# First attention of a two-layer model: scores and maxima on column tiles of 32

## The chip, the cores and the metric

The kernel runs on one core of a Trainium2 chip. The metric is device time in microseconds (us) of one execution, the median of several. TensorE multiplies matrices, VectorE (DVE) reduces and combines, ScalarE (ACT) does exponentials and copies, GpSimd (POOL) small work, and SyncE (SP) issues most DMAs. TensorE's results go to PSUM, which has 8 banks of 128 partitions x 512 f32.

## The reference, cut to what matters

The model has two layers; the change lies in the first layer's attention, over 4 batches of 1024 tokens, 16 heads of 8 dimensions.

```python
zn = (z - mu) / jnp.sqrt(var + EPS) * ln_scale + ln_bias
qkv = zn @ w_qkv
...
scores = jnp.einsum('bhqd,bhkd->bhqk', q, k) / SCALING      # SCALING = 8 ** 0.5
att = jax.nn.softmax(scores, axis=-1)
out = jnp.einsum('bhal,bhlv->bhav', att, v)
out = jnp.transpose(out, (0, 2, 1, 3)).reshape(b, n, d)
out = out @ w_proj + b_proj
return z + out
```

So there are 64 score matrices (4 batches x 16 heads) of 1024 x 1024. Behind this stand a gate, a second layer with a landmark attention and an iterated inverse, and a mixture of eight experts.

## The kernel before

**Operands.** q and k are each split into three bf16 parts; a product of scores is a bf16 matmul whose contraction runs over all nine pairs of parts (ROWS = 72 rows, 9 x 8). A tile of q or k, `q0[c]` or `k0[c]` (b_q, b_k), holds four heads (a "quad") with 96 rows; three slots c take turns. Rows 72 to 74 of q hold the negated row maxima, as three bf16 parts, against rows of ones in k, so that the matmul of scores over XROWS = 75 rows gives score minus maximum. A second pair of tiles, `qo` and `ko` (b_qo, b_ko), holds the two odd heads of a quad once more, on partitions 64 to 127.

**Two heads at a time.** The work runs over 32 duos d (a duo is two heads) and in each over TB = 8 blocks kb of 128 keys. I call one (d, kb) a group; `times_v` uses the same word. Per group TensorE does three things:

- *scores* (L725): four matmuls of 75 x 128 keys against 512 queries, into banks 5, 6 and 7 in turn. Matmul n waits until the exponential of n - 3 is done. ACT's exponential (L670) writes each into a ring b_exp_ring of 12 places.
- *values* (`times_v`, L701) for the group before: four matmuls, one for each 32 partitions of bank 4, f32, weights of 32 columns (8 values, 8 ones, 16 unused). They wait for the fourth exponential of their group. In a duo's first one they also wait until ACT has copied the last duo's sums out of bank 4 (`evacuate`, L662), which ACT does behind the fourth exponential of the new duo.
- *items* (`item`, `maxima_scores`, L556 and L557): the maxima are worked out more than one duo ahead. An item is 128 queries of two heads against 512 keys: the even head's product over rows 0 to 63 of q0 and k0 and the odd head's over partitions 64 to 127 of qo and ko, two matmuls on the two halves of the array's rows, into two banks; DVE takes the maxima of both (L612, 128 x 1024). Item n waits until DVE is done with item n - 2, as there are two pairs of banks. A duo has 16 such items and one more, a transpose of its 16 maxima (L687), whose result DVE negates and splits (L621, L623), and SP stores into rows 72 to 74 of q.

**Order.** It is written out by hand. A group stands on TensorE as scores 0, 1, 2, values of the group before, score 3, then the group's items: two, and three in group kb = 5 (T_GROUP), where the transpose is the first of the three. `upto(d, kb)` counts the items. The first 25 items stand ahead of the first scores.

**Loads.** `load_quad` moves a quad with 13 DMAs (LOADS0): per part q0, k0, qo and ko, and the values once.

Of the kernel before, what the change touches and what calls it, by code (L numbers as in the profile page):

```python
# [6 lines left out]
BF16 = mybir.dt.bfloat16  # L7
# [5 lines left out]
P = 128  # L13
B, T, D, H, HD = 4, 1024, 128, 16, 8
# [4 lines left out]
NPART = 3  # L19
ROWS = NPART * NPART * HD  # L20
# [143 lines left out]

SLOTS = 3
DUOS = 2 * QUADS
MROWS = 64
MAXES = 2 * TB
ITEMS = MAXES + 1
LATE = 2  # L170
# [4 lines left out]
RECS = B - 1  # L175
PROJECT_AT = (0, 1, 2, 3)
E_RING = 12
DISP_ROW = CAP * ROW // 5
DISP_PIECES = -(-DISP_ROW // 2048)
PIECES = DISP_PIECES + ENTRIES * D // P // 2048  # L180
SOONER, LATER = range(2), range(2, NPART + 1)
ZERO_AT = [2 * i for i in range(DISP_PIECES)] + [2 * (QUADS - SLOTS) + 1 + i for i in range(PIECES - DISP_PIECES)]
LOADS0 = 16 * (4 * NPART + 1)
STORED = (48, 48, 32)


# [8 lines left out]
def layer0_inputs(g):  # L195
# [3 lines left out]
    keep = lambda name, shape, dt=F32: g.tiles0.enter_context(nc.sbuf_tensor(name, shape, dt))  # L199
    g.q0 = [keep(f"b_q{c}", [KROWS, HQ, T], BF16) for c in range(SLOTS)]  # L200
    g.k0 = [keep(f"b_k{c}", [KROWS, HQ, T], BF16) for c in range(SLOTS)]
    g.qo = [keep(f"b_qo{c}", [P, HQ // 2, T], BF16) for c in range(SLOTS)]
    g.ko = [keep(f"b_ko{c}", [P, HQ // 2, T], BF16) for c in range(SLOTS)]
    g.v0 = [keep(f"b_v{c}", [P, HQ * P + 2 * HD]) for c in range(SLOTS)]
    part = [[keep(f"a_{c}{i}", [P, T], BF16) for i in range(NPART)] for c in "qk"]
    vs = keep("a_vs", [P, H, TB, 2 * HD])
# [23 lines left out]
    with nc.Block() as block:  # L230
# [177 lines left out]
        @block.tensor  # L408
        def _(pe):
            def transposed_x(b):  # L410
                pe.wait_ge(sem("a_xn"), (b + 1) * TB)
                if b >= 1:
                    pe.wait_ge(sem("a_vs"), b)
                for t in range(TB):
                    last = nc.tensor.transpose(D0[:, t * P:(t + 1) * P], g.XN[:, b * TB + t, :], g.ident[:, :])
                last.then_inc(sem("a_xT_ps"), 1)

            def transposed_z(b):
                pe.wait_ge(sem("a_zn"), (b + 1) * TB)
                if b >= 1:  # L420
                    pe.wait_ge(sem("a_sigr"), b)
                for t in range(TB):
                    last = nc.tensor.transpose(D1[:, t * P:(t + 1) * P], znb[:, t, :], g.ident[:, :])
                last.then_inc(sem("a_zT_ps"), 1)

            def first_maxima(lo, hi):

                for n in range(lo, hi):
                    if n >= 2:
                        pe.wait_ge(sem("b_max_done"), n - 1)  # L430
                    maxima_scores(g, g.q0[0], g.k0[0], g.qo[0], g.ko[0], n, 0, n).then_inc(sem("b_max_scores"), 1)

            pe.wait_ge(sem("ident_set"), 1)
            pe.wait_ge(sem("w_loaded"), 16 * 10)
            for i in range(3):
                nc.tensor.transpose(g.bank(4)[:, i * P:(i + 1) * P], wrkv[:, i, :], g.ident[:, :])
            nc.tensor.transpose(g.bank(4)[:, 3 * P:3 * P + E], wg, g.ident[0:E, 0:E])
            nc.tensor.transpose(g.bank(5)[:, 0:E * HC], b1raw, g.ident[0:E * HC, 0:E * HC])\
              .then_inc(sem("wT_ready"), 1)
            transposed_x(0)  # L440
            transposed_z(0)
            pe.wait_ge(sem("w_ready"), 1)
            for b in range(B):
                now, before = xnT[:, 1:T + 1], xnT[:, 0:T]
                pe.wait_ge(sem("a_znT"), b + 1)
                if b >= 1:
                    pe.wait_ge(sem("a_relu"), b)
                wide(nc, D2, g.wqkv0[:, 0, :], znT[:, :]).then_inc(sem("a_qk"), 1)
                if b >= 1:
                    pe.wait_ge(sem("a_prod"), b)  # L450
                wide(nc, D3, g.wqkv0[:, 1, :], znT[:, :]).then_inc(sem("a_qk"), 1)
                pe.wait_ge(sem("a_xnT"), b + 1)
                rows_times(nc, D0, znT, g.wqkv0[:, 2, :]).then_inc(sem("a_v"), 1)
                pe.wait_ge(sem("a_res"), 2 * b + 1)
                for h in range(T // BANK):
                    s = slice(h * BANK, (h + 1) * BANK)
                    nc.tensor.matmul(D2[:, s], g.wk2[0][:, :], now[:, s], start=True, stop=False)
                    last = nc.tensor.matmul(D2[:, s], g.wk2[1][:, :], before[:, s], start=False, stop=True)
                last.then_inc(sem("a_kk"), 1)
                for t in range(TB):  # L460
                    dst = D1[:, t * P:(t + 1) * P]
                    nc.tensor.matmul(dst, now[:, t * P:(t + 1) * P], g.wr2[0][:, :], start=True, stop=False)
                    last = nc.tensor.matmul(dst, before[:, t * P:(t + 1) * P], g.wr2[1][:, :], start=False, stop=True)
                last.then_inc(sem("a_r"), 1)
                if b + 1 < B:
                    transposed_x(b + 1)
                else:
                    pe.wait_ge(sem("b_loaded0"), LOADS0)
                    pe.wait_ge(sem("a_vs"), B)
                    first_maxima(0, 1)  # L470
                pe.wait_ge(sem("a_kact"), b + 1)
                pe.wait_ge(sem("a_res"), 2 * b + 2)
                rows_times(nc, D3, kaT, g.wvT[:, :]).then_inc(sem("a_kv"), 1)
                if b + 1 < B:
                    transposed_z(b + 1)
                else:
                    pe.wait_ge(sem("a_sigr"), B)
                    first_maxima(1, FIRST)
# [52 lines left out]
def load_quad(g, sp, quad, c, parts=range(NPART + 1)):  # L531

    def moved(dst, src):
        sp.dma_start(dst, src).then_inc(g.sem(f"b_loaded{c}"), 16)

    for m in parts:
        if m == NPART:
            moved(g.v0[c][:, 0:HQ * P], g.v_ops[quad, :, :, :].rearrange("p h n -> p (h n)"))
            continue
        lo = NPART * HD * ((m + 2) % NPART)  # L540
        n = min(NPART * HD, MROWS - lo) // HD
        flat = "h i d t -> (i d) h t"
        moved(g.q0[c][lo:lo + NPART * HD, :, :], g.q_ops[quad, :, :, :, :].rearrange(flat))
        moved(g.k0[c][lo:lo + NPART * HD, :, :], g.k_ops[quad, :, m:m + NPART, :, :].rearrange(flat))
        odd = slice(MROWS + lo, MROWS + lo + n * HD)
        moved(g.qo[c][odd, :, :], g.q_ops[quad, 1:HQ:2, 0:n, :, :].rearrange(flat))
        moved(g.ko[c][odd, :, :], g.k_ops[quad, 1:HQ:2, m:m + n, :, :].rearrange(flat))


FIRST = 5  # L550


def maxima_scores(g, q, k, qo, ko, n, p, i):

    t, keys = slice(i // 2 * P, i // 2 * P + P), slice(i % 2 * BANK, i % 2 * BANK + BANK)
    g.nc.tensor.matmul(g.bank(2 * (n % 2)), q[0:MROWS, 2 * p, t], k[0:MROWS, 2 * p, keys], start=True, stop=True)  # L556
    return g.nc.tensor.matmul(g.bank(2 * (n % 2) + 1), qo[MROWS:P, p, t], ko[MROWS:P, p, keys], start=True, stop=True)  # L557


def max_items():  # L560
# [10 lines left out]
def layer0_attention(g):  # L571
# [19 lines left out]
        sm = sb("d_small", [P, 5, TB])  # L591
    t1, xc = (ap[:, :].rearrange("p (n d) -> p n d", d=D) for ap in (num, den))
    g.tiles0.close()
    q, k, v, qo, ko, mx = g.q0, g.k0, g.v0, g.qo, g.ko, g.mx
    s8, mu8, ss8, v8, rstd8 = (sm[:, i, :] for i in range(5))
    S = g.bank(0, 2)
    tiles = lambda ap: ap.rearrange("p (n c) -> p n c", c=P)
# [5 lines left out]
    with nc.Block() as block:  # L603
# [73 lines left out]
        def _(pe):  # L677
            def item(n):
                d, i = seq[n]
                s, p = d // 2 % SLOTS, d % 2  # L680
                if i == 0 and p == 0 and d:
                    pe.wait_ge(sem(f"b_loaded{s}"), LOADS0 * (d // 2 // SLOTS + 1))
                if n >= 2:
                    pe.wait_ge(sem("b_max_done"), n - 1)
                if i is None:
                    pe.wait_ge(sem("b_m"), d + 1)
                    nc.tensor.transpose(g.bank(2 * (n % 2))[0:MAXES, 0:P], m[:, d % 2, :], g.ident[:, :])\  # L687
                      .then_inc(sem("b_max_scores"), 1)
                    return
                maxima_scores(g, q[s], k[s], qo[s], ko[s], n, p, i).then_inc(sem("b_max_scores"), 1)  # L690

            def times_v(group):

# [21 lines left out]
            for d in range(DUOS):  # L715
                s, p = d // 2 % SLOTS, d % 2
                pe.wait_ge(sem("b_m_loaded"), 16 * NPART * (d + 1))
                for kb in range(TB):
                    if d == DUOS - 1 and kb in PROJECT_AT:
                        project_piece(PROJECT_AT.index(kb))  # L720
                    for i in range(4):
                        n, h, half = 4 * (TB * d + kb) + i, 2 * p + i // 2, i % 2
                        if n >= 3:
                            pe.wait_ge(sem("b_exp_done"), n - 2)
                        nc.tensor.matmul(g.bank(5 + n % 3), k[s][0:XROWS, h, kb * P:(kb + 1) * P],  # L725
                                         q[s][0:XROWS, h, half * BANK:(half + 1) * BANK],
                                         start=True, stop=True).then_inc(sem("b_scores"), 1)
                        if i == 2 and d + kb:
                            times_v(TB * d + kb - 1)
                    for n in range(upto(d, kb - 1), upto(d, kb)):  # L730
                        item(n)
            times_v(TB * DUOS - 1)

# [1267 lines left out]
```

## Time and profile before

| | us |
|---|---|
| runs | 1369.0, 1369.03, 1373.72 |
| median | 1369.03 |
| span of the profiled execution | 1372.0 |
| TensorE busy in it | 1249.1 |
| DVE busy | 1009.4 |
| ACT busy | 851.8 |

The profile has no time of its own for the profiled execution beside its span: from the first to the last instruction 1372.0 us, 1.7 below the slowest and 3.0 above the median of the runs. In views of instructions, PE is a matmul and PEld its load of weights; a row with x8 joins eight in a row, its time from the first start to the last end. The first attention takes the stretch from about 95 to 813 us.

### The profile page before, as it was taken

How to read it: one execution, taken by the hardware profiler on the slowest of the kernel's cores; microseconds unless marked ns; L12 is line 12 of the kernel's file. 1: busy time of each engine (PE TensorE's matmuls, PEld its weight loads, DVE VectorE, ACT ScalarE, POOL GpSimd, SP SyncE). 2: the span in 40 equal slices, each digit the busy share in tenths (PEclk: the TensorE clock that was granted, in tenths of full speed). 3: DMA queues.
4: the chain of work that ended last, by engine and by line, in shares of the span. 5: the costliest groups of instructions: out<-in, count | busy, mean ns of one | idle time of the engine just before them, and what ended most of it. 6: DMA issues, size and time to landing. Idle time of an engine off the chain costs nothing. (4 is left out here: it accounts for less than half of the span.)

```text
span 1372.0 us, 25967 instructions
## 1 busy us (share of the span) xinstructions
PE 1249.1 (91%) x10305; PEld 580.1 (42%) x10305; DVE 1009.4 (74%) x1288; ACT 851.8 (62%) x1447; POOL 237.5 (17%) x309
## 2 busy tenths in 40 slices
PE   6968999999999999999999978998899899899980
PEld 4631222222222222222222225555699566688870
DVE  6878898998899989998999737665676588623324
ACT  3533888888888888888888866555421366533431
POOL 4200110000000000000000002000385222135560
PEclk9986999999999999999999989998999599999995
DMA  5763033232323313222231121100011111123316
GB/s 147 202 199 79 26 65 64 50 76 45 74 64 82 76 40 78 51 66 66 50 74 40 69 71 48 47 16 16 17 31 39 55 44 36 46 69 102 100 58 188
DMA packets 75204, 94.96 MB, mean 69 GB/s; under 512 B 13236, under 2 KB 44684, under 8 KB 74052
## 3 DMA queue, kind: packets, MB, share of 16 engines
q1 hardware_dynamic: 69996, 83.19, 23.9%
q0 software_dynamic: 5088, 10.12, 2.4%
q8 instruction: 81, 1.33, 0.4%
q14 instruction: 39, 0.32, 0.1%
HBM read 54.30 MB, written 38.56 MB: 68 GB/s over the span
## 5 line engine op out<-in xcount | busy, mean ns | idle before, releaser
L670 ACT ACTIVATE b_exp_ring<-psum 128x512 f32<-128x512 f32 x1024 | 555.6, 600 | 148.8 <-PE psum L725 145.6
L612 DVE TENSOR_REDUCE b_mx<-psum 128x2 f32<-128x1024 f32 x507 | 595.8, 1218 | 66.5 <-PE psum L557 65.4
L725 PE MATMUL psum<-b_q,b_k 75*128 75x512 bf16 x1024 | 312.4, 387 | 1.5 <-ACT b_exp_ring L670 1.5
L701 PE MATMUL psum<-b_exp_ring,b_v 128*32 128x512 f32 x2048 | 274.5, 608 | 0.9 <-ACT b_exp_ring L670 0.7
L725 PEld LDWEIGHTS psum<-b_q,b_k 75*128 75x128 bf16 x1024 | 79.3, 97 | 317.0 <-ACT b_exp_ring L670 221.8
L556 PE MATMUL psum<-b_k,b_q 64*128 64x512 bf16 x512 | 168.9, 395 | 25.5 <-DVE b_mx L612 10.6
L557 PE MATMUL psum<-b_ko,b_qo 64*128 64x512 bf16 x512 | 168.9, 395 | 0.0
L740 POOL CAST b_neg<-b_neg_rest 16x128 bf16<-16x128 f32 x32 | 8.9, 279 | 639.6 <-DVE b_neg_rest L623 639.6
L1834 ACT ACTIVATE e_hT<-psum,e_b 128x358 f32<-128x358 f32 (+3 forms) x96 | 53.6, 559 | 75.4 <-PE psum L1854 72.0
L556 PEld LDWEIGHTS psum<-b_k,b_q 64*128 64x128 bf16 x512 | 44.7, 93 | 128.6 <-DVE b_mx L612 41.4
L701 PEld LDWEIGHTS psum<-b_exp_ring,b_v 128*32 128x32 f32 x2048 | 41.3, 108 | 108.6 <-issue 106.0
L1764 POOL DMA_INDIRECT y_tok<-e_y,e_dest x72 | 70.8, 984 | 70.7 <-DVE e_y L1806 51.5
L1274 POOL DMA_INDIRECT x_disp<-x_norm,row_sent x64 | 63.3, 989 | 91.3 <-PE psum L1632 81.3
L1864 PE MATMUL psum<-e_w,e_hT 128*128 128x128 f32 (+1 forms) x576 | 67.4, 277 | 0.0
L1864 PEld LDWEIGHTS psum<-e_w,e_hT 128*128 128x128 f32 (+1 forms) x576 | 64.6, 184 | 1.8
L1612 ACT ACTIVATE f_le<-f_lx 128x1024 f32<-128x1024 f32 x32 | 33.8, 1057 | 47.4 <-DVE f_lx L1574 47.4
L1000 DVE TENSOR_REDUCE c_nm<-psum 128x1 f32<-128x1024 f32 x32 | 37.7, 1220 | 32.2 <-PE psum L1157 32.1
L1854 PE MATMUL psum<-e_xT,e_w 128*128 128x358 f32 (+3 forms) x192 | 60.2, 468 | 0.9 <-DVE e_xT L1778 0.9
L1568 DVE TENSOR_REDUCE f_max<-psum 128x16 f32<-128x1024 f32 x32 | 39.2, 1224 | 24.4 <-PE psum L1632 23.5
L1104 ACT ACTIVATE c_en<-psum,c_nm 128x1024 f32<-128x1024 f32 x32 | 35.7, 1116 | 32.8 <-DVE c_nm L1000 32.8
L1450 PE MATMUL psum<-i_x,i_az 64*64 64x64 f32 x1536 | 47.0, 218 | 1.6 <-DVE i_x L1381 1.5
L1182 PE MATMUL psum<-ident,c_en 128*128 128x128 f32 x256 | 36.7, 289 | 12.2 <-ACT c_en L1104 8.4
(278 smaller groups left out, 1427.6 us busy)
## 6 DMA issues: line engine op xcount, KB each, us to landing
b_q<-q_ops SPq DMA_DIRECT2D x48, 192.0 KB
b_k<-k_ops SPq DMA_DIRECT2D x48, 192.0 KB
k_ops<-a_k SPq DMA_DIRECT2D x20, 256.0 KB, 3.3
x_disp<-b_zeros SPq DMA_DIRECT2D x13, 320.0 KB
e_x<-x_disp SPq DMA_DIRECT2D x8, 520.0 KB
v_ops<-a_vs SPq DMA_DIRECT2D x4, 1024.0 KB, 5.1
b_v<-v_ops SPq DMA_DIRECT2D x16, 256.0 KB
av_out<-b_acc SPq DMA_DIRECT2D x128, 32.0 KB, 1.7
```

Source lines behind the costliest of these rows:

```text
L556: g.nc.tensor.matmul(g.bank(2 * (n % 2)), q[0:MROWS, 2 * p, t], k[0:MROWS, 2 * p, keys], start=True, stop=True)
L557: return g.nc.tensor.matmul(g.bank(2 * (n % 2) + 1), qo[MROWS:P, p, t], ko[MROWS:P, p, keys], start=True, stop=True)
L612: nc.vector.reduce_max(mx[:, d % 2, :, i // 2, i % 2], pair, AX.X).then_inc(sem("b_max_done"), 1)
L670: act.activation(ex[:, n % E_RING, :], g.bank(5 + n % 3), ACT.Exp, scale=ATT_SCALE)\
L701: last = nc.tensor.matmul(AV[32 * i:32 * i + 32, :], v[s][:, at_v:at_v + 32], ex[:, (4 * group + i) % E_RING, :], start=(kb == 0), stop=(k ...
L725: nc.tensor.matmul(g.bank(5 + n % 3), k[s][0:XROWS, h, kb * P:(kb + 1) * P], q[s][0:XROWS, h, half * BANK:(half + 1) * BANK], start=True, ...
L1274: pool.indirect_dma_start(g.x_disp[:, :], bass.IndirectOffsetOnAxis(g.rows_out[:, n:n + 1], 0), g.XNW[:, n % NT, :], None).then_inc(g.sem( ...
L1450: last = nc.tensor.matmul(out[half, i, :], lhs(n * GR + i, half), rhs(n * GR + i, half), start=True, stop=True)
L1764: pool.indirect_dma_start(g.y_tok[:, :], bass.IndirectOffsetOnAxis(dest[c][0:r, t:t + 1], 0), y[c][0:r, t, :], None).then_inc(sem(f"e_sent ...
L1834: act.activation(hT[c][:, i, lo:hi], g.ps[:, (3 + n % 3) * BANK:(3 + n % 3) * BANK + hi - lo], ACT.Gelu, bias=b1[c][:, i:i + 1]).then_inc( ...
L1854: nc.tensor.matmul(g.ps[:, (3 + n % 3) * BANK:(3 + n % 3) * BANK + hi - lo], w1[c][:, i * P:(i + 1) * P], xT[:, lo:hi], start=True, stop=T ...
L1864: last = nc.tensor.matmul(g.ps[0:r, col:col + D], hT[c][:, i, t * P:t * P + r], w2[c][:, i, :], start=(i == 0), stop=(i == HC - 1))
```

## The change

- Scores: each matmul of 128 keys becomes four (STRIPS) of 32 keys, each on its own 32 columns of the array and its own 32 partitions of the bank, all four reading the same 512 queries.
- Maxima: each head's product of 128 queries becomes four of 32 queries, over all 72 rows, and both heads come from q0 and k0. An item is now eight matmuls.
- qo and ko, and their loads, are gone: `load_quad` issues 7 DMAs in place of 13.
- Order in a group: score 0, the first item, score 1, values of the group before, scores 2 and 3, the remaining items.

```diff
-LOADS0 = 16 * (4 * NPART + 1)
+LOADS0 = 16 * (2 * NPART + 1)
...
-        odd = slice(MROWS + lo, MROWS + lo + n * HD)
-        moved(g.qo[c][odd, :, :], g.q_ops[quad, 1:HQ:2, 0:n, :, :].rearrange(flat))
-        moved(g.ko[c][odd, :, :], g.k_ops[quad, 1:HQ:2, m:m + n, :, :].rearrange(flat))
...
-def maxima_scores(g, q, k, qo, ko, n, p, i):
-
-    t, keys = slice(i // 2 * P, i // 2 * P + P), slice(i % 2 * BANK, i % 2 * BANK + BANK)
-    g.nc.tensor.matmul(g.bank(2 * (n % 2)), q[0:MROWS, 2 * p, t], k[0:MROWS, 2 * p, keys], start=True, stop=True)
-    return g.nc.tensor.matmul(g.bank(2 * (n % 2) + 1), qo[MROWS:P, p, t], ko[MROWS:P, p, keys], start=True, stop=True)
+def maxima_scores(g, q, k, n, p, i):
+
+    keys = slice(i % 2 * BANK, i % 2 * BANK + BANK)
+    for x in range(2):
+        for j in range(STRIPS):
+            t = i // 2 * P + 32 * j
+            last = g.nc.tensor.matmul(g.bank(2 * (n % 2) + x)[32 * j:32 * j + 32, :], q[0:ROWS, 2 * p + x, t:t + 32],
+                                      k[0:ROWS, 2 * p + x, keys], start=True, stop=True)
+    return last
...
-                        nc.tensor.matmul(g.bank(5 + n % 3), k[s][0:XROWS, h, kb * P:(kb + 1) * P],
-                                         q[s][0:XROWS, h, half * BANK:(half + 1) * BANK],
-                                         start=True, stop=True).then_inc(sem("b_scores"), 1)
-                        if i == 2 and d + kb:
+                        for j in range(STRIPS):
+                            keys = slice(32 * j, 32 * j + 32)
+                            last = nc.tensor.matmul(g.bank(5 + n % 3)[keys, :],
+                                                    k[s][0:XROWS, h, kb * P + 32 * j:kb * P + 32 * j + 32],
+                                                    q[s][0:XROWS, h, half * BANK:(half + 1) * BANK],
+                                                    start=True, stop=True)
+                        last.then_inc(sem("b_scores"), 1)
+                        if i == 0:
+                            for n in range(upto(d, kb - 1), min(upto(d, kb - 1) + 1, upto(d, kb))):
+                                item(n)
+                        if i == 1 and d + kb:
                             times_v(TB * d + kb - 1)
-                    for n in range(upto(d, kb - 1), upto(d, kb)):
+                    for n in range(upto(d, kb - 1) + 1, upto(d, kb)):
                         item(n)
```

TensorE, an ordinary group of the kernel before, from its last item to the next group's first: scores at L725 (three, then one), values at L701, an item at L556 and L557.

```order
L725 MATMUL psum<-b_q,b_k 128x512 x3
L701 MATMUL psum<-b_exp_ring,b_v 32x512 x4
L725 MATMUL psum<-b_q,b_k 128x512
L556 MATMUL psum<-b_k,b_q 128x512
L557 MATMUL psum<-b_ko,b_qo 128x512
L556 MATMUL psum<-b_k,b_q 128x512
L557 MATMUL psum<-b_ko,b_qo 128x512
```

The same in the changed kernel, with scores at L725 (x4 is one score, x8 two), values at L699 and an item as eight matmuls at L553.

```order
L725 MATMUL psum<-b_q,b_k 32x512 x4
L553 MATMUL psum<-b_k,b_q 32x512 x8
L725 MATMUL psum<-b_q,b_k 32x512 x4
L699 MATMUL psum<-b_exp_ring,b_v 32x512 x4
L725 MATMUL psum<-b_q,b_k 32x512 x8
L553 MATMUL psum<-b_k,b_q 32x512 x8
```

One item has moved to stand behind score 0, and the values stand behind score 1 where they stood behind score 2.

TensorE, group kb = 5 of the kernel before, with the transpose of the maxima at L687, and the start of the group behind it.

```order
L725 MATMUL psum<-b_q,b_k 128x512
L687 MATMUL psum<-ident,b_m 16x128
L556 MATMUL psum<-b_k,b_q 128x512
L557 MATMUL psum<-b_ko,b_qo 128x512
L556 MATMUL psum<-b_k,b_q 128x512
L557 MATMUL psum<-b_ko,b_qo 128x512
L725 MATMUL psum<-b_q,b_k 128x512 x3
L701 MATMUL psum<-b_exp_ring,b_v 32x512 x4
```

The same two groups in the changed kernel, the transpose at L685.

```order
L725 MATMUL psum<-b_q,b_k 32x512 x4
L685 MATMUL psum<-ident,b_m 16x128
L725 MATMUL psum<-b_q,b_k 32x512 x4
L699 MATMUL psum<-b_exp_ring,b_v 32x512 x4
L725 MATMUL psum<-b_q,b_k 32x512 x8
L553 MATMUL psum<-b_k,b_q 32x512 x16
L725 MATMUL psum<-b_q,b_k 32x512 x4
L553 MATMUL psum<-b_k,b_q 32x512 x8
L725 MATMUL psum<-b_q,b_k 32x512 x4
```

The transpose now stands alone behind score 0, the other two items of the group stand together at its end (x16), and between them and the next group's first item stands a single score.

## Rows read from the trace of the kernel before

**Rows 1.** The page: its first line, and busy time of each engine.

```profile
span 1372.0 us, 25967 instructions
PE 1249.1 (91%) x10305; PEld 580.1 (42%) x10305; DVE 1009.4 (74%) x1288; ACT 851.8 (62%) x1447; POOL 237.5 (17%) x309
```

**Rows 2.** The page's costliest groups: busy, mean ns | idle before, and its releaser.

```profile
L670 ACT ACTIVATE b_exp_ring<-psum 128x512 f32<-128x512 f32 x1024 | 555.6, 600 | 148.8 <-PE psum L725 145.6
L612 DVE TENSOR_REDUCE b_mx<-psum 128x2 f32<-128x1024 f32 x507 | 595.8, 1218 | 66.5 <-PE psum L557 65.4
```

**Rows 3.** Stretches (us): time, PE, PEld, DVE, ACT, POOL busy, PE clock, DMA share, GB/s.

```profile
343.00:515.00 172.00, 168.81 (x1024) 40.88 (x1016) 155.72 (x153) 140.23 (x262) 8.00 (x20) 1.00 0.30 67
...
1006.00:1026.00 20.00, 20.00 (x680) 20.00 (x678) 15.32 (x24) 3.32 (x6) 15.34 (x18) 1.00 0.15 45
95.00:113.00 18.00, 9.18 (x31) 1.55 (x29) 17.71 (x18) 0.46 (x1) 1.68 (x3) 0.50 0.55 110
116.00:127.00 11.00, 11.00 (x38) 1.78 (x36) 6.34 (x6) 5.81 (x11) 0.00 (x0) 0.50 0.71 140
```

**Rows 4.** Timeline of PE over one ordinary group: start, time, what.

```profile
617.50 1.07 PE L701 MATMUL psum<-b_exp_ring,b_v 128*32 128x512 f32 x8
618.50 0.39 PE L725 MATMUL psum<-b_q,b_k 75*128 75x512 bf16 x1
618.83 0.39 PE L556 MATMUL psum<-b_k,b_q 64*128 64x512 bf16 x1
...
619.06 0.39 PE L556 MATMUL psum<-b_k,b_q 64*128 64x512 bf16 x1
...
619.38 0.82 PE L725 MATMUL psum<-b_q,b_k 75*128 75x512 bf16 x3
620.13 0.64 PE L701 MATMUL psum<-b_exp_ring,b_v 128*32 128x512 f32 x4
```

**Rows 5.** Timeline of PE around the transpose; last row, the first values of a duo.

```profile
612.63 0.39 PE L725 MATMUL psum<-b_q,b_k 75*128 75x512 bf16 x1
612.86 0.27 PE L687 MATMUL psum<-ident,b_m 128*16 128x128 f32 x1
613.17 0.39 PE L556 MATMUL psum<-b_k,b_q 64*128 64x512 bf16 x1
...
613.82 0.39 PE L556 MATMUL psum<-b_k,b_q 64*128 64x512 bf16 x1 [0.26 <-DVE b_neg_rest L623]
...
601.15 1.06 PE L701 MATMUL psum<-b_exp_ring,b_v 128*32 128x512 f32 x8
```

**Rows 6.** Timeline of ACT around the copy of bank 4 (L662) in two duos.

```profile
600.42 0.59 ACT L662 ACTIVATE b_acc<-psum 128x512 f32<-128x512 f32 x1
...
619.81 1.58 ACT L670 ACTIVATE b_exp_ring<-psum 128x512 f32<-128x512 f32 x3 [0.28 <-PE psum L725]
621.56 0.60 ACT L670 ACTIVATE b_exp_ring<-psum 128x512 f32<-128x512 f32 x1 [0.17 <-PE psum L725]
622.05 0.59 ACT L662 ACTIVATE b_acc<-psum 128x512 f32<-128x512 f32 x1
```

**Rows 7.** Timeline of DVE from the transpose's results to an ordinary group.

```profile
613.48 0.28 DVE L623 SCALAR_TENSOR_TENSOR b_neg_rest<-psum,b_neg 16x128 f32<-16x128 f32 x1
...
619.26 2.36 DVE L612 TENSOR_REDUCE b_mx<-psum 128x2 f32<-128x1024 f32 x2 [0.25 <-PE psum L557]
```

**Rows 8.** All copies of bank 4: count, least, median and most ns, first and last start.

```profile
L662 ACT ACTIVATE b_acc<-psum x32: 592/592/597, 144.5 to 812.7; 128x512 f32<-128x512 f32 x32
```

**Rows 9.** Timeline of PE in a later stage: seven sets of four f32 matmuls on column tiles.

```profile
1100.27 0.97 PE L1661 MATMUL psum<-f_lT,f_sums 128*32 128x128 f32 x28
```

**Rows 10.** Timeline of PE in the last duo, which has no items.

```profile
802.29 1.07 PE L701 MATMUL psum<-b_exp_ring,b_v 128*32 128x512 f32 x8
...
804.37 0.39 PE L725 MATMUL psum<-b_q,b_k 75*128 75x512 bf16 x1 [0.26 <-ACT b_exp_ring L670]
804.69 1.06 PE L701 MATMUL psum<-b_exp_ring,b_v 128*32 128x512 f32 x8
```

More of the change, by code:

```diff
@@ L166 @@
 DUOS = 2 * QUADS
-MROWS = 64
 MAXES = 2 * TB
@@ L177 @@
 E_RING = 12
+STRIPS = P // 32
 DISP_ROW = CAP * ROW // 5
@@ L201, in layer0_inputs @@
     g.k0 = [keep(f"b_k{c}", [KROWS, HQ, T], BF16) for c in range(SLOTS)]
-    g.qo = [keep(f"b_qo{c}", [P, HQ // 2, T], BF16) for c in range(SLOTS)]
-    g.ko = [keep(f"b_ko{c}", [P, HQ // 2, T], BF16) for c in range(SLOTS)]
     g.v0 = [keep(f"b_v{c}", [P, HQ * P + 2 * HD]) for c in range(SLOTS)]
@@ L430, in first_maxima @@
                         pe.wait_ge(sem("b_max_done"), n - 1)
-                    maxima_scores(g, g.q0[0], g.k0[0], g.qo[0], g.ko[0], n, 0, n).then_inc(sem("b_max_scores"), 1)
+                    maxima_scores(g, g.q0[0], g.k0[0], n, 0, n).then_inc(sem("b_max_scores"), 1)
             pe.wait_ge(sem("ident_set"), 1)
@@ L540, in load_quad @@
         lo = NPART * HD * ((m + 2) % NPART)
-        n = min(NPART * HD, MROWS - lo) // HD
         flat = "h i d t -> (i d) h t"
@@ L593, in layer0_attention @@
     g.tiles0.close()
-    q, k, v, qo, ko, mx = g.q0, g.k0, g.v0, g.qo, g.ko, g.mx
+    q, k, v, mx = g.q0, g.k0, g.v0, g.mx
     s8, mu8, ss8, v8, rstd8 = (sm[:, i, :] for i in range(5))
@@ L689, in item @@
                     return
-                maxima_scores(g, q[s], k[s], qo[s], ko[s], n, p, i).then_inc(sem("b_max_scores"), 1)
+                maxima_scores(g, q[s], k[s], n, p, i).then_inc(sem("b_max_scores"), 1)
             def times_v(group):
```

## The prediction, made before the changed kernel ran

> **What bounds the kernel now.** I read the page first: TensorE is busy in 91% of the span, and more than DVE or ACT [rows 1]. The stretches say it for the first attention alone: between 343 and 515 us PE is busy for 168.81 of 172.00 us, DVE for 155.72 and ACT for 140.23, at full clock [rows 3]. So TensorE's order sets the time there, and DVE runs close behind. The groups agree: DVE's maxima take 595.8 us in all and wait for 66.5, ACT's exponentials take 555.6 and wait for 148.8 [rows 2]; both wait for PE.
>
> Then the timeline, for one group. Values start at 617.50, the single score at 618.50, items at 618.83 and 619.06, three scores at 619.38, the next values at 620.13: 2.63 us [rows 4]. One score costs 0.215 when another precedes it (three in 0.82, the last lasting 0.39: two steps in 0.43). Against this, score to item is 0.33, item to score 0.32, three scores to values 0.75 where 3 x 0.215 is 0.645. So each change of kind costs about 0.10. For values to score I have only 1.00; the two passes of an f32 matmul should be 0.43 each: the later stage's sets of 128 columns start (0.97 - 0.27) / 6 = 0.117 apart, its first step included [rows 9], and four times that is at most 0.47. With 0.86 for the values, 0.14 is left for the change and the slower first step.
>
> A duo takes 622.05 - 600.42 = 21.63 [rows 6]; 8 groups are 21.04, so the transpose and its wait cost 0.59. Over all, 32 copies of bank 4 from 144.5 to 812.7 [rows 8] give 21.55 for the mean.
>
> **The change part by part.** *Streams.* All matmuls but the transpose now work on 128 x 32 tiles, so the four changes of kind in a group go (4 x 0.10, and 0.04 of first steps, 0.44). But the item had used both halves of the array's rows at once: two heads in 0.22 (618.83 to 619.06 is 0.23). Now each head is a set of its own over all rows, two sets of 0.216, and two items in a group cost 0.86 instead of 0.45. That hands nearly all of it back. New group: 4 scores and 4 maxima sets, 8 x 0.216 = 1.73, and values 0.86, together 2.59. Gain 0.04 a group, 0.32 a duo. The trace has no set of four bf16 column tiles. Its bounds: below, 0.215, one full bf16 matmul, as each tile must still take 512 columns; above, four in sequence, 0.86. I take 0.216, as the f32 sets on the same tiles do run four abreast (eight matmuls of the values end within 1.07, where one alone lasts 0.59) [rows 4]. The next nearest row is the pair on two halves, 0.23; that is a rival below.
>
> *Issue.* A group now has 40 matmuls and 40 weight loads in 2.6 us, 32 ns each. Between 1006 and 1026 us PE takes 680 and 678 in 20.00 us [rows 3], 15 ns each. So issue is covered.
>
> *Transpose.* It stands between scores, with a change of kind on either side: 0.10 + 0.21 + 0.10 = 0.41. By DVE's order it comes about 0.07 early and waits for that. In sum 0.48 instead of 0.59: gain 0.11.
>
> *The values' wait for bank 4, new.* Set a group's score 0 at 0. Then item at 0.22, score 1 at 0.65, values 0.86, score 2 at 1.72, score 3 at 1.94, item 2.15, next score 0 at 2.59. ACT starts 0.43 behind a score (PE 619.38, ACT 619.81) and takes one each 0.48 when behind: score 2's exponential at 2.17, score 3's at 2.65, the copy of bank 4, 0.49 behind (622.05 after 621.56), at 3.14, done 0.59 later at 3.73 [rows 4, 6]. Copy end to values is 0.14 (600.42 + 0.59 = 601.01, values at 601.15) [rows 5, 6]: 3.87. The values' turn in the second group is at 2.59 + 0.86 = 3.45. Before, scores 0 to 2 and their changes filled this to within about 0.04. So PE stands for 0.42 once a duo, and score 2 and the item behind it stand with it. I take 0.41.
>
> *The two items at the end of group kb = 5, new.* An item waits for DVE's end with the last but one. There the items are: transpose, then X at 2.15 of that group's schedule, Y behind it, and in the next group Z behind score 0. Z needs X's maxima. X's second set starts 0.22 after X, DVE 0.43 + 0.02 later (PE 618.83, DVE 619.26), its 128 x 1024 lasts 1.22, DVE to PE takes 0.06 (DVE ends 613.76, PE goes at 613.82) [rows 2, 4, 5, 7]: 1.95 after X's start. Z's turn is Y (0.43) + score 0 (0.22) + X itself (0.43) = 1.08 after it. The wait is 0.87; I take 0.85. It can't be hidden by an earlier start of X, which needs its own bank and stands behind two scores and the values. Elsewhere DVE takes two items in 2 x 1.14 = 2.28 (2.36 for two, less 1.22) of 2.59, and the first item's turn comes about 0.15 after the bank is free [rows 7].
>
> *Loads.* 96 DMAs fewer on SP. Nobody on PE waited for one; the DMA share is 0.30 [rows 3]. Nothing gained, nothing lost.
>
> *Sum of a duo.* 21.63 - 0.32 - 0.11 + 0.41 + 0.85 = 22.46, 0.83 more; for 30 duos (1 to 30) 24.9.
>
> *Ends.* The last duo has no items. Before, a group took 804.69 - 802.29 = 2.40 [rows 10], tied to ACT. Now the values must wait for score 3's exponential with only two scores between: from score 2, 0.43 + 0.48 + 0.60 + 0.14 + 0.86 = 2.51. Eight groups cost 0.9. The first stretch is at half clock: between 95 and 113 us PE is busy 9.18 of 18.00 with items for a DVE that is full (17.71), and to 127 the clock stays at 0.50 though PE is then busy throughout [rows 3]. An item at half clock costs 0.86 on PE within DVE's 1.14, a turn some 0.04 longer: 25 items, 1 us, and 1 us for the first groups. Or PE's fuller items bring the clock back before the scores begin, and the first three groups save 5 us. I set this at 0 with -5 and +2 for its ends.
>
> So the profiled span becomes 1372.0 + 24.9 + 0.9 = 1397.8, and as the median lies 3.0 below the profiled span, **1395 us**.
>
> **The rivals.** *The two waits don't show* (faster). Place: Z's turn behind kb = 5, and the second group's values. It decides itself at 1.08 against 1.95 us and at 3.45 against 3.87; only if ACT or DVE turned round 0.4 to 0.8 us sooner than now would the streams' gain stand alone: 21.63 - 0.43 - 0.07 = 21.13, 30 x 0.50 = 15 us less, 1372.0 - 15 + 0.9 - 3.0 = 1355. Against it: the turn-rounds are read directly. With one of the waits gone, 1369 or 1382. Also, changes of kind may have cost more than I read.
>
> *A bf16 set takes longer than one matmul* (slower). Four streams read the same 512 columns of b_q or b_k four times, at twice the columns per time of the f32 sets. If a set cost 0.231, as the pair on two halves does [rows 4], 8 x 0.015 x 256 = 31 us more: 1426. In sequence it would be 0.65 x 8 x 256, 1.3 ms more. For it: nothing in the trace shows the form; against it: the f32 sets. The Trainium skill's page "TensorE: Matmul & The Clock Gate", section "Measured speedup vs the span model", gives three column tiles 2.38 times the speed, not 3. As an estimate from that page, a set would cost 1.26 of a matmul and the kernel some 115 us more, near 1510; no row here shows that for bf16, and the f32 rows speak against it.
>
> *The change hands nothing back*: sets run as forecast, but PE was not the bound. That falls with 168.81 of 172.00.
>
> **How the numbers follow.** Forecast 1395 (1388 to 1402): 0.70. Longer sets 0.14, most at 1403 to 1430. Both waits hidden 0.09, one hidden 0.05, 0.02 for sets in sequence. The range is 1377 to 1427; it leaves out the hidden waits and the far end of the long sets. A difference of 0.5% (7 us) is about what a measurement of this kernel can tell from no change. Faster 0.11, same 0.06, slower 0.83.
>
> **What would show it.** Starts of the copies of bank 4 22.4 to 22.5 apart (right), 21.1 (waits hidden), over 22.9 (long sets). Steps between sets 0.216. PE idle for 0.8 us before the first item behind kb = 5, released by DVE's maxima, and 0.4 before the second group's values, released by ACT's copy; before, neither. PE's first groups at 0.50 or 1.00 clock. The forecast is wrong if those idle times are absent, or if scores' steps exceed 0.22.

## The result and the profile after

The changed kernel takes 1397.28 us (median of 4 runs, 1396.07 to 1398.78) against 1369.16: a ratio of 1.020 with a 95% interval of 1.018 to 1.022. It is slower by 28 us. The prediction said 1395 us (range 1377 to 1427), and gave "slower" a chance of 0.83.

The page of the changed kernel, its first line and busy times (to [rows 1]); then three stretches with the columns of [rows 3].

```profile
span 1396.2 us, 38159 instructions
...
PE 1259.7 (90%) x16449; PEld 714.9 (51%) x16449; DVE 1010.3 (72%) x1288; ACT 844.0 (60%) x1447; POOL 237.9 (17%) x309
```

```profile
343.00:515.00 172.00, 164.47 (x2459) 72.32 (x2457) 150.96 (x148) 134.50 (x254) 7.32 (x18) 1.00 0.25 57
95.00:113.00 18.00, 14.96 (x117) 2.54 (x121) 16.04 (x17) 1.15 (x1) 2.27 (x3) 0.50 0.37 81
116.00:127.00 11.00, 10.71 (x108) 3.39 (x108) 8.30 (x8) 4.64 (x9) 0.00 (x0) 0.58 0.60 126
```

PE runs 2.4 times as many matmuls in the middle stretch, at full clock, but is *less* busy than before: 164.47 of 172.00 us against 168.81. Something stands between its matmuls that was not there. The copies of bank 4 (L660) give the length of a duo, as L662 did in [rows 6] and [rows 8]: first the count and first and last start of all, then two of them in ACT's timeline.

```profile
L660 ACT ACTIVATE b_acc<-psum x32: 597/605/606, 146.1 to 839.8; 128x512 f32<-128x512 f32 x32
```

```profile
617.92 0.61 ACT L660 ACTIVATE b_acc<-psum 128x512 f32<-128x512 f32 x1
...
640.34 0.60 ACT L660 ACTIVATE b_acc<-psum 128x512 f32<-128x512 f32 x1
```

A duo takes 640.34 - 617.92 = 22.42 us where it took 21.63. Now the timeline of PE in the changed kernel, from the end of a duo's first group into its second (to [rows 4]).

```profile
616.94 0.60 PE L553 MATMUL psum<-b_k,b_q 72*32 72x512 bf16 x8
617.38 0.39 PE L725 MATMUL psum<-b_q,b_k 75*32 75x512 bf16 x4
617.60 0.60 PE L553 MATMUL psum<-b_k,b_q 72*32 72x512 bf16 x8
618.03 0.38 PE L725 MATMUL psum<-b_q,b_k 75*32 75x512 bf16 x4
618.67 1.06 PE L699 MATMUL psum<-b_exp_ring,b_v 128*32 128x512 f32 x8 [0.26 <-ACT b_acc L660]
619.53 0.64 PE L725 MATMUL psum<-b_q,b_k 75*32 75x512 bf16 x8
619.96 0.64 PE L553 MATMUL psum<-b_k,b_q 72*32 72x512 bf16 x8
620.39 0.43 PE L725 MATMUL psum<-b_q,b_k 75*32 75x512 bf16 x4
620.61 0.64 PE L553 MATMUL psum<-b_k,b_q 72*32 72x512 bf16 x8
621.05 0.42 PE L725 MATMUL psum<-b_q,b_k 75*32 75x512 bf16 x4
621.26 0.64 PE L699 MATMUL psum<-b_exp_ring,b_v 128*32 128x512 f32 x4
```

From values to values it is 621.26 - 618.67 = 2.59. A score is followed by an item after 0.22 (620.39 to 620.61), an item by a score after 0.43, values by a score after 0.86: nothing is lost between kinds any more. But score 1 at 618.03 should have been followed by the values at 618.25, and they start at 618.67, when ACT's copy of bank 4 (617.92 + 0.61 = 618.53) is done. The 0.26 in brackets counts from the modelled end of the score (618.03 + 0.38); counted from the turn of the values, which is what a start-to-start reading gives, the wait is 0.42. The second wait, at the groups kb = 5 and 6 of the same duo:

```profile
628.18 0.43 PE L725 MATMUL psum<-b_q,b_k 75*32 75x512 bf16 x4
628.54 0.28 PE L685 MATMUL psum<-ident,b_m 128*16 128x128 f32 x1
628.75 0.40 PE L725 MATMUL psum<-b_q,b_k 75*32 75x512 bf16 x4
628.98 1.03 PE L699 MATMUL psum<-b_exp_ring,b_v 128*32 128x512 f32 x8
629.84 0.61 PE L725 MATMUL psum<-b_q,b_k 75*32 75x512 bf16 x8
630.27 1.04 PE L553 MATMUL psum<-b_k,b_q 72*32 72x512 bf16 x16
631.14 0.39 PE L725 MATMUL psum<-b_q,b_k 75*32 75x512 bf16 x4
632.21 0.62 PE L553 MATMUL psum<-b_k,b_q 72*32 72x512 bf16 x8 [0.68 <-DVE b_mx L610]
```

The row with x16 is the pair X and Y; Z is the last row. Z's turn was at 631.14 + 0.22 = 631.36; it starts at 632.21, 0.85 later (the 0.68 in brackets counts from the modelled end again). DVE's own timeline says why: it takes X from 630.93, and X plus Y take it 2.36.

```profile
629.88 0.28 DVE L621 SCALAR_TENSOR_TENSOR b_neg_rest<-psum,b_neg 16x128 f32<-16x128 f32 x1
630.93 2.36 DVE L610 TENSOR_REDUCE b_mx<-psum 128x2 f32<-128x1024 f32 x2 [0.78 <-PE psum L553]
```

DVE had stood idle for 0.78 before, waiting for X, and then PE stood for DVE: DVE is done with X at about 632.15 (630.93 + 1.22), and Z starts at 632.21. X had come too late for Z.

**Where the 24.2 us between the two profiled spans came from**, by the first and last copies and by the copy of duo 29's sums (773.9 before, 797.5 after): up to the first copy 146.1 - 144.5 = 1.6; the next 29 duos 651.4 - 629.4 = 22.0; the last two 42.3 - 38.8 = 3.5; all behind the attention 556.4 - 559.3 = -2.9, in stages that the change doesn't touch.

### The profile page after: what moved, and what is told of

It is laid out like the page before. It is cut to its first block and busy times, and to the rows that moved or that the text cites. A ratio compares the mean times of both kernels' runs of the same rounds, so it can differ in the third digit from the quotient of the medians.

```text
span 1396.2 us, 38159 instructions
## 1 busy us (share of the span) xinstructions
PE 1259.7 (90%) x16449; PEld 714.9 (51%) x16449; DVE 1010.3 (72%) x1288; ACT 844.0 (60%) x1447; POOL 237.9 (17%) x309
## 3 DMA queue, kind: packets, MB, share of 16 engines
q1 hardware_dynamic: 64620, 74.79, 20.2%
## 5 line engine op out<-in xcount | busy, mean ns | idle before, releaser
L668 ACT ACTIVATE b_exp_ring<-psum 128x512 f32<-128x512 f32 x1024 | 548.1, 600 | 183.1 <-PE psum L725 182.5
L725 PE MATMUL psum<-b_q,b_k 75*32 75x512 bf16 x4096 | 366.3, 382 | 1.6 <-ACT b_exp_ring L668 1.6
L553 PE MATMUL psum<-b_k,b_q 72*32 72x512 bf16 x4096 | 321.8, 390 | 31.2 <-DVE b_mx L610 25.6
L699 PE MATMUL psum<-b_exp_ring,b_v 128*32 128x512 f32 x2048 | 270.0, 596 | 8.4 <-ACT b_acc L660 6.9
L725 PEld LDWEIGHTS psum<-b_q,b_k 75*32 75x32 bf16 x4096 | 123.1, 96 | 210.7 <-ACT b_exp_ring L668 137.9
L553 PEld LDWEIGHTS psum<-b_k,b_q 72*32 72x32 bf16 x4096 | 116.1, 96 | 155.8 <-DVE b_mx L610 57.7
L699 PEld LDWEIGHTS psum<-b_exp_ring,b_v 128*32 128x32 f32 x2048 | 61.6, 109 | 62.2 <-ACT b_exp_ring L668 49.2
L1859 PEld LDWEIGHTS psum<-e_xT,e_w 128*128 128x128 f32 x192 | 35.7, 190 | 21.7 <-issue 1.3
```

The lines of the kernel that those rows point to most:

```text
L553: last = g.nc.tensor.matmul(g.bank(2 * (n % 2) + x)[32 * j:32 * j + 32, :], q[0:ROWS, 2 * p + x, t:t + 32], k[0:ROWS, 2 * p + x, keys], st ...
L668: act.activation(ex[:, n % E_RING, :], g.bank(5 + n % 3), ACT.Exp, scale=ATT_SCALE)\
L699: last = nc.tensor.matmul(AV[32 * i:32 * i + 32, :], v[s][:, at_v:at_v + 32], ex[:, (4 * group + i) % E_RING, :], start=(kb == 0), stop=(k ...
L725: last = nc.tensor.matmul(g.bank(5 + n % 3)[keys, :], k[s][0:XROWS, h, kb * P + 32 * j:kb * P + 32 * j + 32], q[s][0:XROWS, h, half * BANK ...
L1859: nc.tensor.matmul(g.ps[:, (3 + n % 3) * BANK:(3 + n % 3) * BANK + hi - lo], w1[c][:, i * P:(i + 1) * P], xT[:, lo:hi], start=True, stop=T ...
```

## The experiments

Two theories stand against each other. Mine: *the order costs, the tiles don't*. The rival: *the tiles cost*, by four times the matmuls and weight loads, or by an item that no longer runs two heads at once, whatever the order.

### One half of the change at a time

The changed kernel with the order of before:

```diff
-                        if i == 0:
-                            for n in range(upto(d, kb - 1), min(upto(d, kb - 1) + 1, upto(d, kb))):
-                                item(n)
-                        if i == 1 and d + kb:
+                        if i == 2 and d + kb:
...
-                    for n in range(upto(d, kb - 1) + 1, upto(d, kb)):
+                    for n in range(upto(d, kb - 1), upto(d, kb)):
```

> The changed kernel with the order of before: column tiles and the shorter loads stay, a group is again scores 0 to 2, values, score 3, items. My theory (the order costs, the tiles gain a little): both waits go, a duo takes 21.63 - 0.43 + about 0.3 (values and scores now follow without the changes of kind, so PE comes closer to waiting for the exponentials and for DVE) = 21.4 to 21.5, so 1362 to 1366 us. Rival (the tiles cost, whatever the order): 1385 us or more.

Measured: 1370.4 us (10 runs), ratio 0.9999 (0.9985 to 1.0012), no change from before; a duo takes 21.55. The rival's 1385 is out: 27 of the 28 us go with the order. But I was 4 to 8 us too low: a duo was 0.05 to 0.15 longer than I said, and the part up to the first copy is 2.5 us longer than before (L660's first start, 147.0, against 144.5). So the tiles give a little (664.5 us between the first and the last copy, against 668.2) and take most of it back ahead of the first copy. What keeps a duo above 8 x 2.59 is DVE: in that run's timeline the transpose and the two items behind it, which both wait for DVE, take 1.41 (613.69 to 615.10) where a pair of items alone takes 0.86, and in three groups of a duo the pair takes 0.92. The timeline of PE of this run shows a full group without a change of kind, again 2.59 (600.30 to 602.89):

```profile
600.30 0.39 PE L725 MATMUL psum<-b_q,b_k 75*32 75x512 bf16 x4
600.52 1.04 PE L553 MATMUL psum<-b_k,b_q 72*32 72x512 bf16 x16
601.38 0.82 PE L725 MATMUL psum<-b_q,b_k 75*32 75x512 bf16 x12
602.03 1.03 PE L699 MATMUL psum<-b_exp_ring,b_v 128*32 128x512 f32 x8
602.89 0.39 PE L725 MATMUL psum<-b_q,b_k 75*32 75x512 bf16 x4
```

The kernel before with the new order alone (the same lines, added to it):

> The kernel before, tiles and loads untouched, in the new order. My theory: two more changes of kind in each group (score to item and item to score in the middle, 2 x 0.10 x 256 = 51 us) and the same two waits, less what they overlap: about 23.6 to 23.8 us a duo, 1425 to 1435 us. Rival (the order is neutral or a help, and only the tiles cost): 1369 us or less.

Measured: 1436.88 us, ratio 1.0486 (1.0468 to 1.0503), 23.71 a duo: the duo as said, the time 2 us above my range. The order costs 67 us on the old tiles and 27 on the new (1397.28 less 1370.4): the two halves aren't independent. On the old tiles an item in the middle brings two more changes of kind, as its timeline shows:

```profile
600.64 0.39 PE L725 MATMUL psum<-b_q,b_k 75*128 75x512 bf16 x1
600.97 0.39 PE L556 MATMUL psum<-b_k,b_q 64*128 64x512 bf16 x1
...
601.29 0.39 PE L725 MATMUL psum<-b_q,b_k 75*128 75x512 bf16 x1
```

0.33 and 0.32 where 0.22 would be the work. The new tiles make the new order cheaper, but on neither kind of tiles is it faster than the old one.

### The two waits, one at a time

Changed kernel, the second group's values one score later:

```diff
-                        if i == 1 and d + kb:
+                        if i == (2 if kb == 1 else 1) and d + kb:
```

> The changed kernel with the values of the second group of each duo behind score 2 instead of score 1, nothing else. My theory: the wait for the copy of bank 4 (0.4 us a duo) shrinks by the 0.22 of the score put ahead of it, 30 x 0.21 = 6.5 us less than the changed kernel, 1391 us. Rival (the time is lost elsewhere, ACT catches up anyway): 1397 us, no change.

Measured: 1394.43 us, ratio to before 1.019 (1.0169 to 1.0211), and 22.21 a duo instead of 22.42: 0.21 less, as said. The runs' medians differ by only 3 us. Between the first and the last copy of the profiled executions it is 687.8 against 693.7, so 5.8 less; 0.3 is given back ahead of the first copy and 1.1 behind the last. The intervals of the two ratios overlap (the changed kernel's is 1.018 to 1.022), so it is the duo's length, not the time of the whole kernel, that tells my theory from the rival.

Changed kernel, ACT's copy two exponentials earlier:

```diff
-                    if u == 3 and d:
+                    if u == 1 and d:
```

> The changed kernel with ACT's copy of bank 4 behind the second exponential of a duo instead of the fourth; TensorE's order is untouched. My theory (the second group's values stand because the copy comes late): the copy now starts when the last values are in, 1.9 us into the duo, and pushes the third and fourth exponential back, so the values wait for the fourth exponential instead, about 0.15 in place of 0.42: 22.42 - 0.27 = 22.15 us a duo and 1389 us. Rival (it is the exponential, not the copy, for which they wait): 22.42 or more, 1397 us.

Measured: 1391.06 us, ratio to before 1.0146 (1.0129 to 1.0163), 22.13 a duo (0.29 less). TensorE's program is the same to the last instruction, so the time was ACT's copy. From score 1 to the values of the second group it is now 0.36 (768.22 to 768.58), 0.14 above the score's 0.22: the wait that I had put at 0.15. In the table of who waits for L660, "PE psum L699: 6.9, 27" of the changed kernel is gone, and the copy itself now waits for the last values (last row: idle time of ACT before it, us, and times):

```profile
L660 ACT ACTIVATE b_acc<-psum x32: 597/597/598, 144.9 to 830.9; 128x512 f32<-128x512 f32 x32
...
  PE psum L699: 9.8, 31
```

Changed kernel, Z one score later:

```diff
-                        if i == 0:
+                        if i == (1 if kb == 6 else 0):
```

> The changed kernel with the first item of group kb = 6 (Z of the prediction) behind score 1 instead of score 0. My theory (Z waits 0.85 for the maxima of X, and TensorE stands): score 1 is done in that wait, 0.22 less a duo, 22.20, and 1390 us; the idle time before Z shrinks from 0.84 to 0.62. Rival (the wait only moves into the next group, where the item again comes too soon behind Z): 22.42 a duo, 1397 us.

Measured: 1394.21 us, ratio to before 1.0168 (1.0151 to 1.0185), 22.21 a duo: 0.21 less, and the idle time before Z fell from 0.68 to 0.47 (I had written 0.84 and 0.62, counted from the turn and not from the modelled end):

```profile
627.33 0.61 PE L553 MATMUL psum<-b_k,b_q 72*32 72x512 bf16 x8 [0.47 <-DVE b_mx L610]
```

So the wait did not move into the next group, at least for this much of it. Here too the times alone say little: 3 us less than the changed kernel where I had said 7, with intervals that just overlap, while the profiled span is 6.3 less. Each of the three edits gave back, per duo, about what I had said (0.21, 0.29 and 0.21 for 0.21, 0.27 and 0.22); both waits lie on the path.

### Loads

The changed kernel with b_qo and b_ko kept and loaded, and read by nothing:

```diff
-LOADS0 = 16 * (2 * NPART + 1)
+LOADS0 = 16 * (4 * NPART + 1)
...
+        moved(g.qo[c][odd, :, :], g.q_ops[quad, 1:HQ:2, 0:n, :, :].rearrange(flat))
+        moved(g.ko[c][odd, :, :], g.k_ops[quad, 1:HQ:2, m:m + n, :, :].rearrange(flat))
```

> The changed kernel with the tiles of the odd heads kept and loaded as before (13 DMAs a quad, 8.4 MB more), though nothing reads them. My theory: loads cost nothing here, 1397 us and 22.42 a duo. Rival (fewer loads had given back part of the loss): slower by 0.5% or more, above 1404 us.

Measured: 1399.94 us, ratio to before 1.0212 (1.0195 to 1.0229), beside 1.020 (1.018 to 1.022) without them, and 22.42 a duo in both. The 8.4 MB are there (83.19 MB on the hardware queue, 74.79 without), and cost nothing that these runs can tell.

### What the tiles are worth where they fit

If a change of kind costs 0.10 and an item on two halves costs half of one on columns, the best mix takes columns for the scores alone: they then share their tiling with the values, and the items keep their pairs. The kernel before, with this in place of its matmul of scores:

```diff
-                        nc.tensor.matmul(g.bank(5 + n % 3), k[s][0:XROWS, h, kb * P:(kb + 1) * P],
-                                         q[s][0:XROWS, h, half * BANK:(half + 1) * BANK],
-                                         start=True, stop=True).then_inc(sem("b_scores"), 1)
+                        for j in range(STRIPS):
+                            keys = slice(32 * j, 32 * j + 32)
+                            last = nc.tensor.matmul(g.bank(5 + n % 3)[keys, :],
+                                                    k[s][0:XROWS, h, kb * P + 32 * j:kb * P + 32 * j + 32],
+                                                    q[s][0:XROWS, h, half * BANK:(half + 1) * BANK],
+                                                    start=True, stop=True)
+                        last.then_inc(sem("b_scores"), 1)
```

> The kernel before with only the scores on column tiles of 32; maxima stay as pairs on the two halves of the rows, order and loads as before. My theory: the changes of kind between scores and values go (2 x 0.10 and their first steps, 0.25 a group) while an item keeps its 0.22: a group takes 2.38 on PE, but DVE needs 2.28 of it and the transpose's wait grows, so about 20.6 us a duo, 1.0 less than before, 1335 to 1345 us. Rival (column tiles cost more than the changes they save): above 1369 us. A second rival (DVE or ACT binds at once): 1355 to 1369 us.

Measured: 1337.66 us, ratio 0.9766 (0.975 to 0.9783), 20.71 a duo. This version beats both kernels, before by 32 us. Its timeline of PE, one group:

```profile
600.70 0.83 PE L728 MATMUL psum<-b_q,b_k 75*32 75x512 bf16 x12
601.36 1.03 PE L702 MATMUL psum<-b_exp_ring,b_v 128*32 128x512 f32 x8
602.22 0.39 PE L728 MATMUL psum<-b_q,b_k 75*32 75x512 bf16 x4
602.55 0.39 PE L557 MATMUL psum<-b_k,b_q 64*128 64x512 bf16 x1
...
602.95 0.39 PE L557 MATMUL psum<-b_k,b_q 64*128 64x512 bf16 x1
...
603.27 0.40 PE L728 MATMUL psum<-b_q,b_k 75*32 75x512 bf16 x4
```

Three scores to values 0.66 (0.75 before), values to score 0.86 (1.00 before): 0.23 a group, 1.8 a duo. Only 0.9 of it shows in the duo. In this group the second item comes 0.40 behind the first instead of 0.23 (0.22 to 0.47 in the others), its load of weights released by DVE's maxima: PE has become fast enough to meet DVE, which has idle time of only 38.9 us in front of its maxima in the whole kernel, against 66.5 in [rows 2].

```profile
L613 DVE TENSOR_REDUCE b_mx<-psum 128x2 f32<-128x1024 f32 x507 | 595.4, 1218 | 38.9 <-PE psum L558 35.7
```

Last, what a change of kind is. In this faster kernel the items were cut into 64 rows x 32 columns, so that all work but the transpose stands on 32 columns and only the rows differ:

```diff
-    t, keys = slice(i // 2 * P, i // 2 * P + P), slice(i % 2 * BANK, i % 2 * BANK + BANK)
...
+    keys = slice(i % 2 * BANK, i % 2 * BANK + BANK)
+    for j in range(STRIPS):
+        t, out = slice(i // 2 * P + 32 * j, i // 2 * P + 32 * j + 32), slice(32 * j, 32 * j + 32)
+        g.nc.tensor.matmul(g.bank(2 * (n % 2))[out, :], q[0:MROWS, 2 * p, t], k[0:MROWS, 2 * p, keys],
+                           start=True, stop=True)
+        last = g.nc.tensor.matmul(g.bank(2 * (n % 2) + 1)[out, :], qo[MROWS:P, p, t], ko[MROWS:P, p, keys],
+                                  start=True, stop=True)
+    return last
```

> The kernel with scores on column tiles and the order and loads of before (1337.7 us, 20.71 a duo), and its items cut into eight matmuls of 64 rows x 32 columns (both heads still on the two halves of the rows). It tells what a change of kind costs. Theory one (any change of tiling, rows or columns, costs 0.10): each item stays at 0.22 to 0.23 between two changes, 20.7 us a duo, 1337 us. Theory two (only a change of the columns costs, and now all work but the transpose is on 32 columns): 0.20 less on TensorE for each group, DVE then binds, 19.9 us a duo, about 1313 us.

Measured: 1346.84 us, ratio to before 0.9817 (0.9801 to 0.9833), 20.93 a duo. Theory two is out. In its timeline score to item is still 0.32 and item to score 0.34:

```profile
600.08 0.39 PE L733 MATMUL psum<-b_q,b_k 75*32 75x512 bf16 x4
600.40 0.39 PE L559 MATMUL psum<-b_k,b_q 64*32 64x512 bf16 x1
...
600.90 0.39 PE L559 MATMUL psum<-b_k,b_q 64*32 64x512 bf16 x1
...
601.24 0.83 PE L733 MATMUL psum<-b_q,b_k 75*32 75x512 bf16 x12
```

A change of the row tiling alone costs the 0.10 as well: theory one. (The 0.50 between the two items, 600.40 to 600.90, is a wait for DVE.) But I had it 10 us too fast. Between the first and the last copy it takes 645.5 us against 639.1, 0.22 a duo; an item cut into eight is 0.02 slower to leave, which I had given no price and which makes 0.16 of the 0.22. Another 4.3 us lie behind the last copy (558.5 against 554.2), where the two kernels are the same.

## Why the prediction was right

- *Streams.* Forecast 2.59 a group and sets of 0.216; measured 2.59 and 0.215 to 0.22. The form that the trace of before didn't show, four bf16 sets abreast reading the same 512 columns, runs at the full rate of one matmul. This was the largest open bound, and the rivals of longer sets fall. The Trainium skill ("TensorE: Matmul & The Clock Gate", section "Measured speedup vs the span model") gives three column tiles 2.38 times the speed; this case's trace does not agree with that for a row of such sets, where four column tiles of bf16 take 0.22 from start to start, the time of one matmul of full width.
- *Values' wait for the copy.* Forecast 0.41, measured 0.42. (The schedule puts score 2's exponential at 2.17, where 1.72 + 0.43 is 2.15; without the slip it gives 0.40.) That it is the copy and not an exponential is shown by moving the copy alone (0.29 back).
- *Z's wait for X.* Forecast 0.85, measured 0.85. That it is on the path is shown by one score put into it (0.21 back).
- *Transpose.* Forecast 0.48, measured 0.36 from score to transpose (628.18 to 628.54), less the score's 0.22, and 0.21 from transpose to score: 0.35. What I had too large is the transpose's own work, 0.21, which I had taken from the 0.31 between transpose and item in the kernel before. That item had been waiting: DVE ended the maxima of its bank at 613.12 (611.90 + 1.22), and it started at 613.17. The run with the order alone shows the transpose between two scores of full width, 0.22 behind one and 0.12 ahead of the other, so without a change of kind on either side (rows below). Two changes, into full width and back, and 0.12 make 0.32. The 0.03 that is left is the forecast wait for DVE: the load of the transpose's weights is released by DVE's maxima here, and in the run with the tiles alone, where it is not, the step is 0.32 (613.37 to 613.69).
- *A duo.* Forecast 22.46, measured 22.42. The measured terms add up to 8 x 2.59 + 0.35 + 0.42 + 0.85 = 22.34; 0.08 is spread over groups that are a little longer than 2.59 (2.60 for most). For 29 duos it was 22.0 us against 24.1: 1.2 from the 0.04 of each, the rest from the four duos in which DVE has other work, three reciprocals and one product of 128 x 1024. Those took 22.02 and 22.36 before and 22.61 and 22.97 after, 0.6 more instead of 0.8; that part of DVE's extra work now falls into waits that were there anyway is my reading, and no run tests it.
- *Last duo.* Here the sum was off. I gave duo 30 the price of the others and the last duo 0.9, together 1.7; they took 3.5 more. The last of the copies' distances is 0.8 longer (19.2 against 18.4), as said. The one before it is 2.7 longer, though no item stands behind its transpose and Z's 0.85 is not in it. The traces show three parts. The values' wait for the copy is there, 0.42. The transpose of the last maxima now stands one score behind the last item and must wait for it: it starts 1.85 behind the score (805.15 to 807.00), where it had been 0.87 (783.49 to 784.36), so 1.0 more. And behind this stand of PE the granted clock falls: it is 0.50 between 808 and 811 us, and 1.00 before 807 and from 812 on. In the run with the loads back PE stands for the same 1.42, the clock stays at 1.00, and the distance is 22.1 instead of 23.1 (rows below). The other runs with this order on these tiles agree: with the values later and with Z later the clock falls to 0.50 at this place as well, and it is 22.9 and 23.1; with the copy earlier it doesn't fall, and it is 21.8. So the clock is 1.0 of the 2.7, and some 0.3 is left without a name. I had neither this wait nor the clock in the sum; why the clock falls behind the same wait in three executions and not in two, the runs don't show.
- *The first stretch.* I had put 0, with -5 and +2 for its ends; it is +1.6 to the first copy, out of two parts. The items ahead of the scores come 2.38 for two at half clock (97.42, 99.80), 1.19 each, where DVE took them every 1.14 before (11 in 12.54 us): the 0.05 more of a turn that I had put at 0.04. DVE is still busy for 5.96 of the 6.00 us from 101 to 107, and PE waits 0.20 for it ahead of every second item. In all the first exponential comes 2.6 us later (119.2 against 116.6). The clock then comes back earlier: 0.58 of full between 116 and 127 us, where it had been 0.50 [rows 3]; that returns 1 us. In the items ahead, between 95 and 113 us, the granted clock is 0.50 in both kernels; PE is busy for 9.18 of 18.00 us of it before and for 14.96 after.

The transpose between scores of full width, in the run with the order alone:

```profile
606.29 0.39 PE L725 MATMUL psum<-b_q,b_k 75*128 75x512 bf16 x1
606.51 0.28 PE L687 MATMUL psum<-ident,b_m 128*16 128x128 f32 x1
606.63 0.38 PE L725 MATMUL psum<-b_q,b_k 75*128 75x512 bf16 x1
```

Duo 30 of the changed kernel, the transpose and the stretch behind it (columns of [rows 3]); the last row is the stretch at the same place in the run with the loads back:

```profile
807.00 0.27 PE L685 MATMUL psum<-ident,b_m 128*16 128x128 f32 x1 [1.42 <-DVE b_m L613]
...
808.00:811.00 3.00, 3.00 (x28) 0.65 (x20) 0.00 (x0) 1.88 (x5) 0.70 (x2) 0.50 0.04 10
...
808.70:811.70 3.00, 2.64 (x36) 0.78 (x32) 0.00 (x0) 2.27 (x5) 0.68 (x2) 1.00 0.04 10
```

The items ahead of the scores, in the changed kernel:

```profile
97.42 2.17 PE L553 MATMUL psum<-b_k,b_q 72*32 72x512 bf16 x16 [0.47 <-DVE b_mx L610]
99.80 2.18 PE L553 MATMUL psum<-b_k,b_q 72*32 72x512 bf16 x16 [0.20 <-DVE b_mx L610]
```

- *Behind the attention* the changed kernel is 2.9 us faster in the profiled execution, and I had nothing there. Other runs of the same later stages spread by as much from the last copy to the end (554.2 us in the run with scores on columns, 561.4 in the run with the order alone), so I put no cause to it.

So the span of 1397.8 that I had worked out, against 1396.2, has errors of -2.1 (the 29 duos), +1.8 (the last two), +1.6 (the first stretch) and -2.9 (behind), as measured less forecast. And the median lies 1.1 above the profiled span, not 3.0 below, which took 1.6 of error to 2.3 on the other side. The 3.0 was no property of the kernel. The changed kernel's profiled execution took 1398.21 us with a span of 1396.2, 2.0 more than its span; with the same 2.0 the profiled execution of the kernel before took about 1374.0, close to the slowest of its runs (1373.72). So the two profiled spans differ by less (24.2) than the medians (28.1). The closeness of 1395 to 1397.28 is in part luck; the terms of the middle are not.

## What to carry to other kernels

Count a TensorE order in streams and in changes of tiling: on this kernel each change between full width, row halves and column tiles cost about 0.10 us, and going between bf16 and f32 on the same tiles cost nothing. Give neighbouring work the same tiling (columns for the scores beside values that need them: 32 us), but don't give up two matmuls abreast for it (with the items on columns too, in the old order, 1370.4 us instead of 1337.7). And before spreading work of a partner engine evenly, walk through the places where the pattern breaks: a pair in a row, a buffer copied once per round, the last item before something that needs them all. In this kernel waits stood at each of them (0.85 and 0.42 a duo, and 1.6 once). And before taking an interval between two starts for the work of the first, look at what the second waited for.

## What was not expected of the hardware

Going from a bf16 score to the f32 values on the same column tiles takes no longer than from score to score (0.21 to 0.22), and with four loads of weights of 32 columns to each set the steps are still 0.215 to 0.22. A change of rows from 128 to 64 with the columns unchanged at 32 costs as much as one of columns (0.32 between starts where 0.22 is work). And a single wait of PE of 1.42 us, in a stretch of full clock, is followed by some 3 us at 0.50 in three profiled executions and by none in two.
